# Ten row buffers instead of six for the expert blocks, and the gathers of the first group's results four places later in GpSimd's order

## The reference

```
x = x + tanh(g_xattn[0]) * L0_xattn(layernorm(x), ctx)      # 64 keys a batch
x = x + tanh(g_ffn[0])   * L0_ffn(layernorm(x))             # 16 experts, the best 2 of a row
x = x + tanh(g_xattn[1]) * L1_xattn(layernorm(x), ctx)      # a linear map and a mean over ctx
x = x + tanh(g_ffn[1])   * L1_ffn(layernorm(x))             # 256 -> 1024 -> 1024 -> 1024 -> 256
```

```
y = (silu(x @ w1[e]) * (x @ w3[e])) @ w2[e]                 # 256 -> 128 -> 256
```

## Time and profile before

| | us |
|---|---|
| three executions | 514.69, 522.88, 517.7 |
| their median | 517.7 |
| span of the profiled execution, first to last instruction | 517.8 |
| stage 1 / stage 2 / stage 3 of it | 69.6 / 103.3 / 344.9 |
| busy in the span: PE, DVE, ACT, POOL | 485.9, 312.4, 214.4, 149.5 |

### The profile page before, as it was taken

One profiled execution on the slowest core, in us unless ns is written; L12 is line 12 of the kernel. 1 busy time (PEld: TensorE's weight loads), 2 busy tenths in 40 slices (PEclk: granted clock), 3 DMA queues, 4 the chain that ended last, 5 costly groups with the idle time before them and its releaser, 6 DMA issues.

```text
span 517.8 us, 7829 instructions
## 1 busy us (share of the span) xinstructions
PE 485.9 (94%) x2750; PEld 417.0 (81%) x2750; DVE 312.4 (60%) x836; ACT 214.4 (41%) x444; POOL 149.5 (29%) x159
## 2 busy tenths in 40 slices
PE   8898978996899889999999999999999999999996
PEld 8697768885789668888987888897888888788886
DVE  3568876673588566557455964626677634645433
ACT  4379914663467676532245121226322123611210
POOL 1867856656762320201062110116011101000000
PEclk9799977998899999999999999999999999999999
DMA  8945833786672548521141121005032002022101
GB/s 296 330 169 161 282 100 100 198 289 181 198 213 84 184 135 281 163 82 41 42 128 57 52 71 42 0 2 162 22 99 64 0 1 81 3 72 70 42 1 47
DMA packets 34465, 58.82 MB, mean 114 GB/s; under 512 B 4529, under 2 KB 18353, under 8 KB 34354
## 3 DMA queue, kind: packets, MB, share of 16 engines
q1 hardware_dynamic: 29760, 47.12, 27.8%
q0 software_dynamic: 3840, 10.49, 7.4%
q10 hardware_dynamic: 818, 0.61, 0.4%
HBM read 47.85 MB, written 14.42 MB: 120 GB/s over the span
## 4 chain that ended last, share of the span: by engine, by line
PE 84%; DVE 7%; issue 2%; ACT 2%; another core or an unknown queue 1%; DMA 1%; POOL 1%; SPq 0%; DVEq 0%; POOLq 0%
PE bank L1987 23%; PE bank L1988 22%; PE bank L1959 5%; PE bank L1956 5%; PE bank L1559 4%; PE bank L1561 4%; PE bank L1560 4%; PE bank L2020 3%; PE bank L2019 3%; PE bank L1805 2%; PE bank L1645 2%; PE bank L1808 1%; DMA gw<-gate 1%; PE bank L1619 1%
## 5 line engine op out<-in xcount | busy, mean ns | idle before, releaser
L1533 ACT ACTIVATE sg<-bank,colv 128x512 f32<-128x512 f32 x64 | 44.1, 690 | 177.2 <-PE bank L1988 177.2
L1987 PE MATMUL bank<-Ah,Wr 128*128 128x512 f32 x256 | 100.3, 392 | 0.4 <-DVE sg L1242 0.4
L1987 PE MATMUL bank<-Bh,Wr 128*128 128x512 f32 x256 | 99.9, 390 | 0.0
L1988 PE MATMUL bank<-Al,Wr 128*128 128x512 f32 x256 | 99.7, 390 | 0.0
L1988 PE MATMUL bank<-Bl,Wr 128*128 128x512 f32 x256 | 99.7, 389 | 0.0
L1559 PE MATMUL bank<-EL,turned 128*128 (+1 forms) x141 | 47.4, 336 | 12.1 <-ACT yb L1465 9.3
L1987 PEld LDWEIGHTS bank<-Ah,Wr 128*128 128x128 f32 x256 | 48.1, 188 | 11.7 <-DVE sg L1242 1.3
L1988 PEld LDWEIGHTS bank<-Bl,Wr 128*128 128x128 f32 x256 | 48.1, 188 | 9.8
L1988 PEld LDWEIGHTS bank<-Al,Wr 128*128 128x128 f32 x256 | 48.1, 188 | 9.8
L1987 PEld LDWEIGHTS bank<-Bh,Wr 128*128 128x128 f32 x256 | 48.1, 188 | 9.8
L1259 DVE CAST Ah<-sg 128x512 fp32r<-128x512 f32 x32 | 13.6, 426 | 60.0 <-ACT sg L1533 60.0
(11 more groups left out here) (280 smaller groups left out, 1031.2 us busy)
## 6 DMA issues: line engine op xcount, KB each, us to landing
Wraw<-panels SPq DMA_DIRECT2D x44, 256.0 KB
stage<-panels SPq DMA_DIRECT2D x44, 256.0 KB
ES<-experts SPq DMA_DIRECT2D x16, 384.0 KB, 4.9
ys_dram<-yb SPq DMA_DIRECT2D x47, 128.0 KB
ys_dram<-x SPq DMA_DIRECT2D x1, 1920.0 KB, 8.4
X<-x SPq DMA_DIRECT2D x3, 512.0 KB, 7.8
xb_dram<-xb SPq DMA_DIRECT2D x3, 512.0 KB, 5.3
out<-outb SPq DMA_DIRECT2D x3, 512.0 KB
```

The lines of the kernel that those rows point to most:

```text
L1533: eng.activation(sg[:, (8 * layer + m) % 3, :], bank[m % 4][:, :], ACT.Gelu, scale=colv[:, c + m:c + m + 1]).then_inc(f_act[m], 1)
L1987: mm(bank[m % 4][:, :], Wr[:, base:base + P], h[0][:, k, :], start=k == 0, stop=False)
L1988: ins = mm(bank[m % 4][:, :], Wr[:, base:base + P], h[1][:, k, :], start=False, stop=k == FK - 1 and not general)
```

## The change

`NXG` goes from 6 to 10. Four new buffers `xg_late` lie over `y2`. A table `XG_ORDER` gives the order in which the buffers are used: as before for the first six, then the new four, so these are used first for blocks 6 to 9. As their place holds routing data, POOL waits before gather 6 until the second one-hot product is done (`pe_perm >= 2`). Gather i now waits for the turning of block i - 10 instead of i - 6. Six semaphores of the expert loads are used again instead of two, so POOL clears four more ahead of the first gather (L613 before, L616 now). `Y_AT`, `ROOT2_AT`, `ROW_AT` and `ROOT3_AT` all move four places later, as far as there are places (46 is the last). PE's, ACT's, DVE's and SP's lists keep their order; only which buffer PE reads differs.

```diff
-Y_AT = (28, 29, 31, 32, 34, 35, 37, 38)
-ROOT2_AT, ROW_AT, ROOT3_AT = (37, 45), (38, 45), (44, 46)
+Y_AT = (32, 33, 35, 36, 38, 39, 41, 42)
+ROOT2_AT, ROW_AT, ROOT3_AT = (41, 46), (42, 46), (46, 46)
...
-NXG = 6
+NXG = 10
+XG_ORDER = (5, 0, 1, 2, 3, 4, 6, 7, 8, 9)
...
-        xg_more = nc.alloc_sbuf_tensor_at("xg_more", [P, NXG - 4, D], F32, offset=wlo_off - 4 * (NXG - 4) * D)
+        xg_more = nc.alloc_sbuf_tensor_at("xg_more", [P, 2, D], F32, offset=wlo_off - 4 * 2 * D)
+        xg_late = nc.alloc_sbuf_tensor_at("xg_late", [P, NXG - 6, D], F32, offset=xn_off + 4 * TG * D)
...
-            b = (i + NXG - 1) % NXG
-            return (xg[:, b, :] if b < 4 else xg_more[:, b - 4, :]), dma_xg[b], 16 * (i // NXG + 1)
+            b = XG_ORDER[i % NXG]
+            rows = xg[:, b, :] if b < 4 else xg_more[:, b - 4, :] if b < 6 else xg_late[:, b - 6, :]
+            return rows, dma_xg[b], 16 * (i // NXG + 1)
...
+                if i == XG_ORDER.index(6):
+
+                    eng.wait_ge(pe_perm, 2)
```

## The result

The changed kernel took 525.17 us (median of 10 runs, 522.83 to 528.73) against 518.5 us (10 runs) of the kernel before: a ratio of 1.014, 95% interval 1.0107 to 1.0174. I had forecast 516.1 us and 510 to 522.5. The time lies outside the range, and the sign is wrong.

A forecast was written before the change was run, and what follows sets the result against it. PE was taken as held by waits for ACT's `yb` and a slow clock in stage 2's middle third, POOL nearly the bound. 517.8 + 0 + 0 - 1.6 = 516.2 us, predicted as 516.1; range 510 to 522.5.

The forecast's parts named there:

- On the path this is worth zero in the first third: Stage 2, first third: gathers from 6 on start earlier, but gathers there were early already, so gain 0.
- the head start: Stage 2: POOL gathers further ahead of PE, from gather 6 at 77.1 until ten ahead, about block 27 at 103.4 us.
- what is left: Middle third, executions without stalls: PE would wait 0.8 to 3.2 us for block 39 with six buffers; gain taken as 1.6 us.
- The block with the least time was not block 19: Block 19's 6.4 us from issue to use taken as shortest found; gathers landed 1.8 us or more before PE wanted them.
- No view tells me why ACT was late there: Middle third: PE's 4.28 and 1.81 us gaps wait for ACT's copy of `yb`; ACT's lateness was called unexplained.
- clearly faster: the large stalls go: Rival, middle third: spreading gathers removes the 4.28 and 1.81 us stalls and 3.5 us of slow clock: 508.2 us; chance 0.10.
- stores land late: Rival, from 98 to 104 us: early gathers and panel loads delay stores, so ACT's copy and PE: 520.4 us; chance 0.18.
- come up at the same moment as before: Middle third: result gathers behind gather 32 still wait for turning 22, so start near 115 as before; DVE's addition unchanged.
- The last gather starts near 148: End of stage 2: the last block gather moves from 156.67 to near 148; nothing on the path.

The follow-up runs named there:

- before_again: The kernel before, unchanged, profiled on chip 6 beside the changed kernel: 506.01 us, span 505.9 us.
- after_again: The changed kernel (ten buffers, places four later) run again on chip 6 against the kernel before: ratio 0.9984.
- ten_oldY: Ten buffers with the full head start, result gathers at their old places, against the kernel before on chip 5: ratio 0.9984.
- after_third: The changed kernel (both halves) run again on chip 1 against the kernel before: ratio 1.0010.
- ten_oldY2: Ten buffers with the full head start, result gathers at their old places, repeated on chip 1 against the kernel before: ratio 1.0009.
- the pairs: Changed kernel, but result gathers in pairs behind block gathers 31, 32, 34 and 36, against the kernel before: 0.9944 on chip 6, 0.9951 on chip 14.
- after: Profile of the changed kernel from its first comparison with the kernel before, chip not known: 525.17 us, ratio 1.014, span 523.4 us.

## Why the prediction was wrong

**"On the path this is worth zero in the first third" is the step that failed.** I priced the head start by what it brings and asked only whether the gathers land in time. In the profile after they did: PE's waits name no gather. But in the first comparison PE's idle time in the first third grew from 1.6 to 7.3 us and its granted clock fell by 0.12, because PE's signals reached ACT up to 7.4 us late and PE stood behind ACT. On chip 13 the ten-buffer half with its head start costs 3.2% alone (1.0317), the stalls of both thirds together; the sum had 0.

**The gain of 1.6 us, "what is left", was too large.** The mechanism exists: in an execution without the large stalls, `before_again`, PE waits for block rows, and no such wait stands in `after_again` beside it. But it is 0.4 us (before 143.12), half of the least that I gave such an execution (0.8 us), and the ratio there was 0.998 with 1 inside its interval. Nor do ten buffers rule such waits out, as I had it: `ten_oldY` has 1.5 us of them. Part of the excess was in the working. POOL's own need of 26.2 us still held the 1.5 us that it waits for stores, so POOL was slower than PE by 5.0 us and not 6.5.

**The block with the least time was not block 19.** The turning at 105.31 is of `xg_more` and belongs to block 18. Block 19, gathered at 98.91, was turned at 106.72 and had 7.8 us. The least is 6.0 us, of block 1 (70.86 to 76.89). That the gathers landed in time in that execution stands, by a margin of 1.4 us instead of 1.8.

**"No view tells me why ACT was late there"** was wrong about the views. ACT's and POOL's timelines of before, side by side, show ACT waiting 3.78 us for a signal of PE's and both going on within 0.4 us of each other at 124, after six gathers without a pause. Had I read it, the first question about a change that makes gathers run without pauses for longer would have been what it does to PE's signals.

**The rival "clearly faster: the large stalls go"** looked at the right place, since these stalls do fall into POOL's crowded stretch, and had the direction wrong: ten buffers do not spread gathers, they string them together. It had 0.10.

**The rival "stores land late"** had the sign and less than half of the size (2.6 us of 6.7), and not the mechanism. In the gap of the first third no store could be late: ACT's first copy waits for none, and the first store went out at 92.80. The 16 DMA engines were busy 0.32 of the time from 87.0 to 92.8. On chip 1 they were at 0.74 in the first third without a stall. The Trainium skill (DMA: Bandwidth & Descriptors, "Issuing engines are not separate DMA queues") says that transfers started by ACT, SP or GpSimd all run on the same 16 engines and interleave there, whichever of them started them. No run here contradicts it, and by these rows it is not what cost the time.

**The result gathers "come up at the same moment as before"** held on the 505 us chips, beside the head start: 112.3 us in `after_third`, 112.2 in `ten_oldY2`. Against the kernel before on the same chip it held to 1.5 us (113.6 in `after_again`, 115.1 in `before_again`). It held on chip 13 between those two kernels as well (120.8 and 121.1). In the first comparison it failed against the kernel before (123.35 against 115.26), where PE was already late. But I charged DVE's fixed places nothing, since DVE's row of before showed no idle time. `before_again` shows 4.6 us of it. With DVE late by the other stall, that limit was hidden in the profile that I had. With six buffers the new places cost 2.2 to 2.4% against it.

**The head start's own timing.** Gather 6 came at 78.19, not 77.1, after 1.61 us of waiting for the one-hot product's signal, which I had taken as given at 75.3. The product ended at 76.24 by its modelled end, so this signal came 1.9 us late, and behind the six gathers with which the kernel before begins too. In `after_again` it ended at 76.28 and gather 6 started at 77.38 without a wait. On chip 1 nothing waited there and gathers ran without a pause for 33 places. I had said until about block 27. "The last gather starts near 148" was 155.12 in the first comparison, and 139.7 to 142.3 in the three profiles of the changed kernel on 505 us chips.

**What stays open.** On one 520 us chip the ten-buffer half is shown to cost 3.2%. In the four profiles of such chips ACT's long waits end inside POOL's runs or within 2.1 us behind them. That the uninterrupted run holds the signals up, and not something else that goes with it, is argued and not shown: no run there puts a pause in, and POOL's runs end on a late signal themselves. Not known is what differs between the two kinds, or how long a run must be (in the kernel before, six gathers stood in front of the stall). Nor is it known how six buffers with the new places, or the pairs, do on a 520 us chip. The pairs, best on two 505 us chips, are therefore no recommendation for all.

## What to carry to other kernels

Deeper buffering can have a price besides memory. It takes away the pauses of the engine that issues the gathers, and here, on some chips, the other engines' signals were late in such stretches. When a wait names engine X, look at what X was waiting for, and put the timelines of all engines beside each other over that gap, above all where the releaser is "remote" or "issue". A gather whose consumer sits at a fixed place of another engine's order should be moved together with that place, and where its issuer in turn waits for work behind that consumer, the delay is paid several times over. And take a small result from several chips before giving it one cause.

## What the runs showed of the hardware

- In stretches in which POOL issued indirect DMAs every 1.25 us, signals of PE reached ACT and POOL late. ACT's longest waits that only a late signal explains were 3.0 to 3.8 us at the ends of runs of six to ten, and 6.40 and 4.68 us at a run of 16. In `after` the signals were 5.7 and 7.4 us behind the modelled ends of their products. This was so in all four profiles of kernels that took 518 to 536 us. In none of those on chips 1, 5, 6 and 14 did ACT or POOL have such a wait, with runs of up to 33 gathers.
- The same kernel before takes 504.14, 506.01, 505.41 and 504.73 us on four chips, and 518.5 and 520.87 us in the other two comparisons, 3% more. That is more than the change is worth on either kind.
- The granted clock of TensorE was 1.00 (2.4 GHz) from 83.5 to 87.0 in `after` and 0.50 (1.2 GHz) from 92.8 to 96.5, after it had stood for 5.90 us.
